# A ring of shared one-hots, a one-word table and longer scatter steps in a graph network kernel

## The reference

```python
x = layernorm(x + GCN(x, src, dst))
x = layernorm(x + ATT(x, src, dst, edge_attr_64))
```

## Time and profile before

| | us |
|---|---|
| median of three runs | 5,244.65 (5,244.09 to 5,247.79) |
| the profiled execution | 5,247.15 |
| its span, first to last instruction | 5,245.6 |
| VectorE busy | 3,410.0 (65%) |
| TensorE busy | 3,828.0 (73%) |
| ScalarE busy | 1,665.9 (32%) |
| GpSimd busy | 3,435.8 (65%) |
| mean granted TensorE clock | 0.942 of full speed |

### The profile page before, as it was taken

One profiled execution on the slowest core, in us unless ns is written; L12 is line 12 of the kernel. 1 busy time (PEld: TensorE's weight loads), 2 busy tenths in 40 slices (PEclk: granted clock), 3 DMA queues, 4 the chain that ended last, 5 costly groups with the idle time before them and its releaser, 6 DMA issues. The chain is left out here.

```text
span 5245.6 us, 95577 instructions
## 1 busy us (share of the span) xinstructions
PE 3828.0 (73%) x24852; PEld 2425.0 (46%) x24853; DVE 3410.0 (65%) x10241; ACT 1665.9 (32%) x4208; POOL 3435.8 (65%) x3648
## 2 busy tenths in 40 slices
PE   5346666666639999999999857676666667676664
PEld 3112222222224454545454436666666666666664
DVE  8999999999921120202020168887887878878787
ACT  0056666666620010101010123333333333333332
POOL 2067777777777777777730017777777777777773
PEclk8889999999969999999999979999999999999998
DMA  9322332322379999898978634444444444444442
GB/s 365 119 85 92 102 128 90 139 90 95 134 185 327 321 310 336 295 337 290 337 270 291 197 105 131 131 131 131 132 132 131 131 130 131 132 131 132 131 131 77
DMA packets 363179, 929.25 MB, mean 177 GB/s; under 512 B 75929, under 2 KB 193549, under 8 KB 361192
## 3 DMA queue, kind: packets, MB, share of 16 engines
q1 hardware_dynamic: 203136, 552.41, 31.6%
q0 software_dynamic: 143520, 317.62, 21.4%
q10 hardware_dynamic: 16400, 57.93, 2.9%
HBM read 727.27 MB, written 200.43 MB: 177 GB/s over the span
## 5 line engine op out<-in xcount | busy, mean ns | idle before, releaser
L749 POOL DMA_INDIRECT records<-recs,poss x1562 | 1626.5, 1041 | 552.8 <-issue 544.0
L1380 POOL DMA_INDIRECT kv<-kv_table,rec x1616 | 1552.5, 961 | 497.4 <-issue 465.4
L909 PE MATMUL ps<-adj,mh 128*128 128x500 f16 (+1 forms) x6370 | 1315.4, 366 | 0.0
L1418 PE MATMUL ps<-msg,ohf 128*128 128x136 f32 x3232 | 504.1, 301 | 636.8 <-DVE msg L1478 635.5
L582 PE MATMUL ps<-h 128*128 128x490 f16 x2500 | 651.5, 385 | 399.4 <-ACT h L683 342.0
L909 PEld LDWEIGHTS ps<-adj,mh 128*128 128x128 f16 x6370 | 619.8, 97 | 686.4 <-issue 35.8
L1063 DVE SCALAR_TENSOR_TENSOR h<-ps,vecs,deg (+1 forms) x65 | 46.7, 718 | 1120.3 <-PE ps L909 1120.3
L537 DVE TENSOR_SCALAR h<-iota,rel 128x490 f16<-128x490 f16 x2500 | 774.0, 370 | 0.0
L1418 PEld LDWEIGHTS ps<-msg,ohf 128*128 128x128 f32 x3232 | 418.8, 196 | 712.8 <-DVE msg L1478 364.4
L582 PEld LDWEIGHTS ps<-h 128*128 128x128 f16 x2500 | 200.7, 99 | 850.3 <-ACT h L683 555.8
L1444 ACT ACTIVATE msg<-scores 128x32 f32<-128x32 f32 x404 | 92.6, 229 | 1288.8 <-DVE scores L1473 1288.8
(11 more groups left out here) (262 smaller groups left out, 4519.6 us busy)
## 6 DMA issues: line engine op xcount, KB each, us to landing
adj<-adj_full SPq DMA_DIRECT2D x420, 875.0 KB, 5.9
adj_full<-blk SPq DMA_DIRECT2D x12, 6125.0 KB
records<-deg ACTq DMA_DIRECT2D x1, 56576.0 KB, 198.1
rec<-records SPq DMA_DIRECT2D x404, 136.0 KB
recs<-in_edge_attr POOLq DMA_DIRECT2D x142, 352.0 KB, 5.6
kv<-kv_table,rec POOLq DMA_INDIRECT x1616
records<-recs,poss POOLq DMA_INDIRECT x1563
adj<-adj_tail SPq DMA_DIRECT2D x35, 437.5 KB, 3.7
```

Source lines behind the costliest of these rows:

```text
L749: G.indirect_dma_start(out=k.rec_d, out_offset=bass.IndirectOffsetOnAxis(ap=k.poss[:, q, j:j + 1], axis=0), in_=k.recs[:, q, j, :], in_off ...
L909: last = mm(bank, mh[:, part, hi, :], adj[:, c, x * width:(x + 1) * width], start=False, stop=True, skip_group_check=True)
L1380: G.indirect_dma_start(out=kv[:, q, j, :], out_offset=None, in_=k.kv_d, in_offset=bass.IndirectOffsetOnAxis(ap=rec[:, q, j, RD:RD + 1].bit ...
L1418: last = mm(PS[:, 6 + q % S, j // 2 * MW:(j // 2 + 1) * MW], ohf[:, q, j, :], msg[:, q, j, :], start=(j % 2 == 0), stop=(j % 2 == 1))
```

## The change

- **Ring.** The `lo` one-hot of a tile is made once, into `ohl`, a ring of 50 tiles (the first three again behind it, so that four in a row never wrap). A two-group stride has 25 tiles; of each group's, ScalarE makes the last six, in three pairs, and VectorE the others, a little over 12 tiles ahead of the windows. TensorE's weights are read at an address that a register holds.
- **One word.** For each group one word for VectorE (the first tile and four differences of three bits) and one for TensorE (five ring places of six bits), each with a flag of its own; ScalarE reads none. The flag is also set where tiles stray too far from their usual place. `code` counts within four windows, so that the `rel` instructions go, and `codes` is 4 x 490 columns wide. The tables come from a running maximum and minimum over the tiles and counts of them, five by VectorE and five by ScalarE.
- **Degrees** are stored to DRAM block by block in the window stage. `psum_free` goes: TensorE waits for `put`.
- **Scatter.** Steps of 22 tiles, two buffers; the next step's load and copies come behind the fifth DMA of a step; 11 rounds of two steps (484 tiles) in the window stage, 1,078 in the convolution.
- **Queries** stay f32 in `k.qn`: one product for each tile in place of three, and the split into parts goes.

The diff, cut to its core:

```diff
-TW = 16
+TW = 24
+RING = 50
+AHEAD_LO = 12
+TWO = 25
+PAIRS = 3
-RR = 4
-SG = 11
+RR = 2
+SG = 22
-SPLIT = 17
+SPLIT = 11
+FETCH = 5
...
+                V.tensor_tensor_scan(least[0:WP, ::-1], tmn[0:WP, ::-1], tmn[0:WP, ::-1], float(N), ALU.min, ALU.min).then_inc(sem("least_ready"), 1)
+                L(V.tensor_tensor_scan(most[0:WP, :], tmx[0:WP, :], tmx[0:WP, :], 0.0, ALU.max, ALU.max))
...
-                    V.scalar_tensor_tensor(m[0:WP, 0:T], tmn[0:WP, 0:T], w4[0:WP, 0, j:j + 1], up[0:WP, 0:T], ALU.is_lt, ALU.mult)
-                    L(V.scalar_tensor_tensor(n[0:WP, 0:T], tmx[0:WP, 0:T], thr[0:WP, j:j + 1], down[0:WP, 0:T], ALU.is_ge, ALU.mult))
-                    V.tensor_reduce(w4[0:WP, 1, j:j + 1], m[0:WP, 0:T], AX.X, ALU.max)
-                    L(V.tensor_reduce(w4[0:WP, 2, j:j + 1], n[0:WP, 0:T], AX.X, ALU.max))
...
+                    V.tensor_scalar(eq[0:WP, j % 2, 0:T], most[0:WP, 0:T], thr[0:WP, j:j + 1], None, ALU.is_lt, ALU.add,
+                                    accum_out=w4[0:WP, 1, j:j + 1]).then_inc(starts, 1)
+                v.wait_ge(starts, WPP)
+                L(V.tensor_tensor(tmx[0:WP, 0:T - 2], most[0:WP, 3:T + 1], least[0:WP, 0:T - 2], ALU.subtract))
+                L(V.tensor_reduce(small[0:WP, 4:5], tmx[0:WP, 0:T - 2], AX.X, ALU.max))
...
+                    nc.scalar.activation(eq[0:WP, 2 + j % 2, 0:T], least[0:WP, 1:T + 1], ACT.Sign, bias=over[0:WP, j:j + 1],
+                                         accum_out=w4[0:WP, 2, j:j + 1]).then_inc(sem("ends_counted"), 1)
...
+                def spread(t, i=None):
+                    slot = t % RING
+                    of_tile = k.lo[:, t:t + 1] if i is None else k.lo[:, bass.ds(i * (2 * TWO) + t, 1)]
+                    for q in (slot, slot + RING) if slot < FAST - 1 else (slot,):
+                        V.tensor_scalar(ohl[:, q * P:(q + 1) * P], codes[:, 0:P], of_tile, None, ALU.is_equal)
...
+                    packed = entry(nc, DVE, k.wt, gr * TW + DWORD, 0, 2 * DLONG)
+                    with v.If(packed < DLONG):
...
-                            last = V.tensor_scalar(rel[:, par, x, :], k.code[:, bass.ds(first[x], FAST)], wbase[:, bass.ds(w + x, 1)], None, ALU.subtract)
-                        last.then_inc(rel_ready, 1)
-                        for x in range(WPP):
-                            q = (q0 + x) % SL
+                            q, f = (w0 + x) % SL, (w0 + x) % PH
+                            if x:
+                                first = v.snap(within(first + ((packed >> (12 - 3 * x)) & 7), T - FAST))
                             v.wait_ge(done, w + x + 1)
-                            lo_onehots(ohl[:, q, 0:JV[x], :], first[x], JV[x])
-                            if x == 0:
-                                v.wait_ge(rel_ready, gr + 2)
                             for j in range(FAST):
-                                last = V.tensor_scalar(ohc[:, q, j, :], iota[:, :], rel[:, par, x, j:j + 1], None, ALU.is_equal)
+                                last = V.tensor_scalar(ohc[:, q, j, :], codes[:, f * WC:(f + 1) * WC], k.code[:, bass.ds(first + j, 1)], None, ALU.is_equal)
                             last.then_inc(ready, 1)
...
                 def group(gr, w0):
-
-                    long = entry(nc, PE, k.wt, gr * TW + 15, 0, 1)
-                    with pe.If(long < 1):
+                    packed = entry(nc, PE, k.wt, gr * TW + PWORD, 0, 2 * PLONG - 1)
+                    pe.wait_ge(ready_lo, gr * PAIRS + PAIRS)
+                    with pe.If(packed < PLONG):
                         for x in range(WPP):
                             w, q = pe.snap(gr * WPP + x), (w0 + x) % SL
-                            pe.wait_ge(psum_free, w + 1)
+                            at = pe.snap(within(((packed & (63 << 6 * x)) << (7 - 6 * x)) if x < 2 else (packed >> (6 * x - 7)) & (63 * P), (RING - 1) * P))
+                            pe.wait_ge(put, w + 1)
                             pe.wait_ge(ready, w + 1)
-                            pe.wait_ge(ready_lo, w + 3)
                             for j in range(FAST):
-                                last = nc.tensor.matmul(PS[:, q, 0:WC], ohl[:, q, j, :], ohc[:, q, j, :],
+                                last = nc.tensor.matmul(PS[:, q, 0:WC], ohl[:, bass.ds(at + j * P, P)], ohc[:, q, j, :],
...
+                def distances(t, i, n):
+                    for j in range(2):
+                        of_tile = k.lo[:, t + j:t + j + 1] if i is None else k.lo[:, bass.ds(i * (2 * GB * TWO // 2) + (t + j), 1)]
+                        last = A.activation(away[:, n, j, :], codes[:, 0:P], ACT.Abs, bias=of_tile, scale=-1.0)
+                    last.then_inc(away_ready, 1)
+
+                def onehots(t, n, nth):
+                    slot = t % RING
+                    assert FAST - 1 <= slot < RING - 1
+                    act.wait_ge(away_ready, nth + 1)
+                    A.activation(ohl[:, slot * P:(slot + 2) * P], away[:, n, :, :].rearrange("p j c -> p (j c)"), ACT.Relu, bias=1.0, scale=-1.0).then_inc(ready_lo, 1)
...
+                        if more:
+                            t = of_act((q if loop is not None else b) * GB + g + 1)[x]
+                            if x == 0:
+                                act.wait_ge(done, (b * GB + g) * WPP + SL)
+                            distances(t, loop, x)
+                        if y == 0:
+                            if i is not None:
+                                act.wait_ge(stored[q], 16 * i)
+                            act.wait_ge(summed, b + 1)
+                        put_window(b * BW + y, q, y, (q * BW + y) % SL)
+                        if more:
+                            onehots(t, x, nth)
...
+                def degree(b, q, width):
+                    sp.wait_ge(deg_free, b + 2)
+                    sp.dma_start(k.deg_d[bass.ds(b * BD, width)].rearrange("(o c) -> o c", o=1), degs[0:1, q, 0:width]).then_inc(deg_moved[q], 16)
...
+    def fetch(step, q):
         g.dma_start(k.recs[:, q, :, 0:F], attr[:, bass.ds(step * SG, SG), :]).then_inc(loaded[q], 16)
+        G.tensor_copy(k.recs[:, q, :, RD:RL + 1].bitcast(I32), k.dl[:, bass.ds(step * SG, SG), :])
+        G.tensor_copy(k.poss[:, q, :], k.pos[:, bass.ds(step * SG, SG)]).then_inc(copied, 1)
...
-        if more:
-            if type(i) is not int or i > 0 or nq == 0:
-                g.wait_ge(sent[nq], 16 * SG * (i + (nq == 0)))
-            load(step + 1, nq)
-        c0 = step * SG
-        G.tensor_copy(k.recs[:, q, :, RD:RL + 1].bitcast(I32), k.dl[:, bass.ds(c0, SG), :])
-        G.tensor_copy(k.poss[:, q, :], k.pos[:, bass.ds(c0, SG)]).then_inc(copied, 1)
...
+            if j == FETCH and more:
+                if type(i) is not int or i > 0 or nq == 0:
+                    g.wait_ge(sent[nq], 16 * SG * (i + (nq == 0)))
+                fetch(step + 1, nq)
...
-                sp.dma_start(k.deg_d.rearrange("(p c) -> p c", p=1), k.deg[0:1, :]).then_inc(deg_moved, 16)
...
-                        for part in range(3):
-                            mm(PS[:, 2 + q % S, j * P:(j + 1) * P], oht[:, q % S, j, :],
-                               k.q3[:, bass.ds(b[j // 2], 1), part, :].rearrange("p a c -> p (a c)"), start=(part == 0), stop=(part == 2))
+                        mm(PS[:, 2 + q % S, j * P:(j + 1) * P], oht[:, q % S, j, :],
+                           k.qn[:, bass.ds(b[j // 2], 1), :].rearrange("p a c -> p (a c)"), start=True, stop=True)
```

361 lines of the change are left out of this document (186 added, 175 removed).

## The result

The changed kernel takes 5,122.28 us (median of four runs, 5,115.41 to 5,124.47) against 5,246.22 for the kernel before beside it (four runs, 5,244.09 to 5,249.86): a ratio of 0.976, 95% interval 0.9744 to 0.9778. It is faster by 124 us, where 295 were forecast; the range, 4,870 to 5,070, does not hold it.

What follows compares the result with a forecast made beforehand. VectorE was taken to bound the window stage. Terms -284 (windows), +3.5 (start), -6 (end), -7 (tables), -2 and +2 (convolution), -2 (projection) summed to -295.5 from 5,247.15: forecast 4,952 us, range 4,870 to 5,070.

Steps and rivals of the forecast that it cites:

- Sign and bound: Whole kernel: faster, chance 0.96; VectorE sets the window stage, busy for 1,106.8 of 1,162 us before the change.
- Work of a window, 785 us: Window stage: VectorE's one-hots cost 1.256 us a window, 785 us for 625 windows.
- interference, 75: Window stage: 484 scatter instructions of GpSimd cost VectorE 0.155 us each, 75 us.
- 0.31 us for a 490-column one-hot: Window stage, expected sign: 2,500 one-hots of 490 columns at 0.31 us on VectorE.
- TensorE and ScalarE pace nothing: Window stage, against the rival that another engine or sequencer paces windows at 1.5 to 1.65 us: 5,062, chance 0.17.
- Of the 55 us idle I keep a third, 18: Window stage: VectorE's idle time falls from 55 to 18 us as it loads fewer words.
- register addresses cost nothing: Window stage: one-hots taking their address from registers add nothing, since `rel` instructions with two such ran at 0.16 us.
- GpSimd quiet from about 1,010: Window stage: 484 tiles, 22 steps of 33 us, scattered after some 730 us, long before the windows end.
- The rival on the other side: Window stage: GpSimd and VectorE exclude each other, VectorE standing 469 us; stage 1,272, kernel 5,346; chance 0.03.
- Tail and handover: Window stage's end: tail store 32.6 plus handover 5.2, 37.8 us against 43.6, so -6.
- Start and tables: Before the windows: start +3.5 us for wider `codes` and one-hots made ahead; tables -7 us.
- the +2: Convolution: the scatter ends 26 us before the stage does and costs only its share of the last round, +2 us.

Runs made afterwards that it cites:

- e11: e9 with the scatter split at 88 tiles in the window stage instead of 396; window stage 848.3 us.
- e9: Changed kernel with VectorE's slow path shortened, 6 empty instructions ahead of its loop, scatter split at 396 tiles; 5,052.1 us, ratio 0.9641 to the kernel before.
- e6: e1 without VectorE's slow path and with 20 empty instructions ahead of its loop; 5,112.4 us, window stage 877.2 us.
- e10: e9 with 12 empty instructions ahead of VectorE's loop in place of 6; 5,115.5 us, window stage 992.5 us.
- e13: e9 split at 484 tiles, one more slow-path wait out, two four-column TENSOR_TENSORs per group of five windows; 4,972.9 us, ratio 0.9483 to the kernel before.
- e16: e13 with one four-column TENSOR_TENSOR per group of five windows in place of two; 4,967.2 us, ratio 0.9466 to the kernel before.
- e14: e13 with its two TENSOR_TENSORs replaced by two four-column 16-bit TENSOR_SCALARs at the same places; 5,037.0 us.
- e1: Control: changed kernel with extra masks on slow-path counts (never entered) and on attention's loop counts; 5,122.2 us, window stage 1,067.6 us.
- e3: e1 with the slow path taken out of TensorE's group; 5,114.6 us, window stage 1,060.7 us.
- e15: e6 with one four-column TENSOR_TENSOR ahead of every window's one-hots, five a group; 4,996.5 us.

## Why the prediction was wrong, point by point

**Sign and bound: right.** VectorE bounds the window stage and the kernel is faster; no transfer or slow path turned it.

**Work of a window, 785 us, and interference, 75: right.** Together 860; VectorE is busy 861.3. The test of the interference (e11 against e9) gave 0.159 us for each scatter instruction against 0.155. Among its signs, 0.31 us for a 490-column one-hot does not follow from its own sum, which makes it (2,500 x 0.257 + 75) / 2,500 = 0.29; it is 708.2 / 2,500 = 0.28. TensorE and ScalarE pace nothing: in e6 the windows follow each other at 1.40 us, the 878 / 625 of the prediction.

**Idle time, "Of the 55 us idle I keep a third, 18": the step that failed.** It measured 199 us (1,060.4 less 861.3), 181 over. That is the whole of what the stage falls short by, 182.5; the kernel falls short by 163, since the smaller parts gave 19 more than forecast. The stops of e10 against e9, and their absence in e6 (stage 877.2), show what it is: the fetch of a loop that touches too many pieces. The prediction costed loads, addresses and waits, which are what the instructions do, and never asked what the instructions weigh. The body of VectorE's loop went from 294 to 393 instructions (29 `lo` one-hots and 26 address operations for them among the new ones), and it came to lie across five pieces in the place of three. That register addresses cost nothing held for the time each takes; their room did not cost nothing. (A one-word load did have a row in the trace of the kernel before: the flag's load, L72, 0.32 us in the median on VectorE.) The instruction packets on the profile's page could not have shown it before the change; that the loop grew by a third could have been counted in the built program.

**"GpSimd quiet from about 1,010": wrong, and it would have been enough to spoil the forecast alone.** The step was 22 times 1.47 us, "33 us with the load": a price taken from a stage in which a TENSOR_TENSOR stood in every window, for a stage from which the change removes it. With the stage at its forecast length (e6) the same 484 tiles last until 1,356, and the kernel takes 5,112. Only with both put right, e13 and e16, does the forecast's region come: 4,973 and 4,967, against 4,952.

**The rival on the other side had the right pair of engines and the wrong loser.** It let VectorE stand for GpSimd; it is GpSimd that stands for VectorE, 5.8 us for an instruction of 0.97. The prediction dismissed the rule of the Trainium skill ("SBUF — State Buffer", "Two separate sides": an exclusive lock held for the whole instruction, the other fully blocks) on VectorE's side of the earlier trace rows, at a time when its run was broken in each window; GpSimd's side stood there too, 1,114 ns for a scatter instruction that takes 960 to 1,020 beside the convolution. By that rule whoever comes first holds the other up; the runs agree for the blocked scatter instructions, and show more than it says: such a one waited not for one instruction of VectorE but for a run of some twenty. They disagree for the 162 of e9's 352 that ran undisturbed beside such a run, and for VectorE, with 0.16 us for one scatter instruction. The same page (section "Who interferes with whom") states that `tensor_scalar` can enter the two-port modes that contend with GpSimd, and that `tensor_tensor` has no such mode, though with both inputs in SBUF it contends with GpSimd's reads. e13 against e14 agrees in its direction (1,148 against 1,736 ns); the tiny TENSOR_SCALARs, which helped against none (1,736 against 2,063), are not explained by it.

**The small parts.** Tail and handover measured 26.7 us, forecast 37.8: the 32.6 of the tail store in the earlier trace rows were taken as its own, but 30 scatter instructions ran beside it, and in the changed kernel, with none beside it, the store lands 25.8 us after its issue. The part is 11 us too dear for lack of an undisturbed row; that the scatter is what lengthened it was not tested by itself. Start and tables together came 3 us better than forecast, which I did not divide further. In the convolution the step of 22 is cheaper than forecast: 1.36 us a tile over the stage against 30.4 / 22 = 1.38, so that the last scatter starts 52 us before the stage's end and not 26. In its last full round the scatter ran on, and the round took 288.1 us as without one: the +2 was nothing.

```profile
2577.30:2865.40 288.10, 282.08 (x1398) 141.85 (x1398) 50.91 (x88) 16.50 (x28) 197.79 (x214) 0.99 0.89 304
```

Projection (-2.8 against -2) and attention (-1.3 against 0) are as forecast; GpSimd's gathers covered the f32 queries.

**What stays open.** What decides whether a scatter instruction beside a run of 490-column one-hots is blocked. Why the fetch of a loop that doesn't fit takes 2 us a stop here and up to 9 in every fifth turn (a block's store runs beside it then, but no run took the store away). TensorE's and ScalarE's loops, too long for any place, are still fetched; blocks of 50 windows take about 68 and 75 us in turn from the fourth on in e6, and I have not found whether that comes from them. And why two tiny TENSOR_SCALARs, and the 128-column ones, let the scatter through where 490-column ones of the same kind do not: their short time is a guess that no run separates.

## What to carry to other kernels

When a change makes a loop's body longer, count its instructions and where they come to lie, the paths that never run included; four empty instructions ahead of the loop were worth 68 us here, over half of what the whole edit had brought. Take an engine's price under contention from a stage with the same neighbours: a removed instruction may have been what let the other engine in. And when a stage gets shorter and the kernel does not, look at once at who is still working after it.

## What the runs showed of the hardware that I had not expected

- VectorE's loop stays loaded if it touches at most three pieces of 128 instructions (8,192 bytes), with edges in this program at 64, 192, 320, 448 and 576, or within one or two instructions of that: 53 to 55 fetches on queue 14 in the whole run. With four pieces 203 or 204 (240 in the kernel before, 90 with three), with five 234 or 235, and 112 to 190 us of a stage of 31 turns (e10 against e9, e1 against e6).
- Each turn fetched 4.8 pieces where the loop touches four, 5.8 where it touches five. The fetches on queue 8 are of 16,384 bytes; they are TensorE's, since they fall from 78 to 61 when its slow path is taken out (e3).
- A one-instruction scatter on GpSimd, 0.97 us by itself, took up to 6.16 us beside an unbroken run of 16-bit TENSOR_SCALARs on VectorE (e11), though not each time, and 1.53 at most with one four-column TENSOR_TENSOR of 0.15 us in each window (e15); VectorE lost 0.16 us to each (e11 against e9).
- A blocked one ended among the short, 128-column TENSOR_SCALARs behind a run of twenty 490-column ones: 71 of 77 in e9, 69 of 78 in e6.
